# Attention over edge pairs: TensorE's two products change places, and VectorE instead of GpSimd copies the row numbers

## The chip, the cores and the metric

The kernel runs on one core of a Trainium2 chip. The metric is the device time of one launch in microseconds, the median of several runs; lower is better.

## The reference

A network of four graph layers on 6250 nodes and 206250 edges, in float32. The change is in the second layer, an attention over edges. For each edge, with features `m1` made from the rows of its two end nodes:

```
a   = sum(leaky(m1_s @ W_alpha).reshape(e, 4, 16) * alpha_dot, -1)     # logits, 4 heads
ex  = exp(a - segment_max(a, dst)[dst]); alpha = ex / segment_sum(ex, dst)[dst]
val = sigmoid(m1_s @ Ws_val), (m1_v @ Wv_val) * sigmoid(... @ Wg)
m2  = tensor_product(val, rsh)
h   = concat(m2_s @ Ws_vlin, m2_v @ Wv_vlin)                            # 4 heads x 40
agg = segment_sum(alpha * h, dst)
```

## The kernel before, in words

`edge_layer1` (phase name `e1`) does this with a running softmax. The edges stand in 1620 tiles of 128, taken as 810 pairs. For each of 12 tiles in turn there is a table in DRAM (`comb`) with a row per node: the node's mapped features, its maximum so far, and its sums so far. For each pair GpSimd gathers four blocks of 128 rows by indirect transfer (`srow` twice by source node, `crow` twice by destination node), and later writes two `crow` blocks back. The row numbers are columns of one int32 list in SBUF (`lists`); a small copy (L1095) puts the six columns of a pair into its slot of the ring `at` first.

Every engine runs the same loop, `run_steps`: a turn has six steps (`SLOTS`), written out, with 135 turns; the first `peel` turns are written out ahead of the loop. At the top of each turn an engine computes register values for its waits. In one step an engine works on several pairs at different stages: `s.back(k)` is the pair k steps older. The order inside a step is written by hand, and engines agree through counting semaphores. The stages of a pair that matter here:

- GpSimd: copy of row numbers in step s (L1095), four gathers one step later (L1076, L1079), two writes back five steps later (L1087), which wait for `kept` and `row_set`.
- VectorE (a = 2, b = 3, c = 4, r = 5 steps back): adds the gathered rows of a (L1320, `mv_set`); logits of b (L1323, L1326, `lg_set`); value products of b (L1331, `vv_set`); features of a (L1338 to L1352); maximum over the scores of b's first tile (L1357, waits for `x_lo`); accumulation of r (L1376, `row_set`); maximum for the second tile (L1394); new maximum (L1400), masks of a (L1406), differences (L1413).
- TensorE (a, b, c = 2, 3, 4 back): weights of a (`weights`, L1114); scores of b's first tile (`scores`, L1124 and L1127); the head maps of c (`second`, L1143 and L1145, 16 matmuls, `h_ps`); transposes of a (`turn`, L1120); scores of the second tile; and so on.

`second` writes PSUM bank `ps_h`, in which part of b's value matmuls (`VALS[1]`) also lie until VectorE has read them; so it waits for b's `vv_set`.

Of the kernel before, what the change touches and what calls it, by code (L numbers as in the profile page):

```python
# [6 lines left out]
I32 = mybir.dt.int32  # L7
# [975 lines left out]
def edge_layer1(nc, g, A, src_table, combs):  # L983
# [10 lines left out]
    def each(n):  # L994
        return [(16 * n, 16 * n * c) for c in (-1, 0, 1)]
    with Phase(nc, "e1") as ph:
        two = range(2)

        def ring(name, n, shape, dtype=F32):
# [3 lines left out]
        WvT, w2, adot = ph.sb("WvT", [64, P]), ph.sb("w2", [P, 2]), ph.sb("adot", [P, 4, 17])  # L1003
        straight, spare = ph.sb("straight", [P, CS]), ph.sb("spare", [P, 4, 16])
        ident16 = ph.sb("ident16", [P, P], BF16)
        keys, yt, at = ring("keys", SLOTS, [P, 2, P]), ring("yt", SLOTS, [P, 2, 10]), ring("at", SLOTS, [P, 6], I32)
        basis, comps = ring("basis", SLOTS, [P, P]), ring("comps", SLOTS, [P, P])
        srow, crow = ring("srow", 3, [P, 2, D]), ring("crow", SLOTS, [P, 2, COMB + 4])

# [13 lines left out]
        wl, made, wready, blank, straightened = (ph.sem(n) for n in ("weights", "made", "wready", "blank", "straightened"))  # L1023
        keys_in, mixed_in, yt_in = ph.sems_of("keys_in", SLOTS), ph.sems_of("mixed_in", SLOTS), ph.sems_of("yt_in", SLOTS)
        srow_in, crow_in, written = g.pool_dmas["e1"]
        (at_set, mixed_set, w_ps, w_read, mv_set, dup_set, cross_set, dots_set, feats1, m1_lo, m1_hi, m1T_lo, m1T_hi, a_ps,
         ra_set, th_set, lw_set, lg_set, vv_set, by_set, feats2, sv2_hi, sv2_lo, m2_lo, m2_hi, m2T_lo, m2T_hi, h_ps, masks, same_set,
         x_lo, x_hi, mx_lo, mx_hi, mn_set, dif_set, ex_set, kept, scaled, hw_set, g_ps, row_set) = (ph.sem(n) for n in (
             "at_set", "mixed_set", "w_ps", "w_read", "mv_set", "dup_set", "cross_set", "dots_set", "feats1", "m1_lo", "m1_hi", "m1T_lo",
             "m1T_hi", "a_ps", "ra_set", "th_set", "lw_set", "lg_set", "vv_set", "by_set", "feats2", "sv2_hi", "sv2_lo", "m2_lo", "m2_hi",  # L1030
             "m2T_lo", "m2T_hi", "h_ps", "masks", "same_set", "x_lo", "x_hi", "mx_lo", "mx_hi", "mn_set", "dif_set", "ex_set", "kept",
             "scaled", "hw_set", "g_ps", "row_set"))
# [1 line left out]
        def landed(n, times, more=0):  # L1034
            return n.value(16 * times, 16 * times * (n.off + 1 + more))

        def steps(eng, step, lag, held=()):
            run_steps(eng, step, lag, SLOTS, GROUPS, COUNTS + list(held))

        with nc.Block() as block:  # L1040
            @block.sync
            def _(sp):
# [23 lines left out]
            @block.gpsimd  # L1066
            def _(pool):
                def step(s):
                    n = s.back(1)
                    if n.exists():  # L1070
                        pool.wait_ge(wl, 16 * 9)
                        pool.wait_ge(at_set, n.count(1))
                        if n.reuses(3):
                            pool.wait_ge(mv_set, n.count(-2))
                        for q in two:
                            pool.indirect_dma_start(out=srow[n.j % 3][:, q, :], out_offset=None, in_=src_table,  # L1076
                                                    in_offset=bass.IndirectOffsetOnAxis(ap=at[n.j][:, q:q + 1], axis=0)).then_inc(srow_in[n.j], 16)
                        for q in two:
                            pool.indirect_dma_start(out=crow[n.j][:, q, 0:COMB], out_offset=None, in_=combs[2 * n.j + q][0:NP, :],  # L1079
                                                    in_offset=bass.IndirectOffsetOnAxis(ap=at[n.j][:, 2 + q:3 + q], axis=0)).then_inc(crow_in[n.j], 16)  # L1080
                    w = s.back(5)
                    if w.exists():
                        pool.wait_ge(wl, 16 * 9)
                        pool.wait_ge(kept, w.count(1))
                        pool.wait_ge(row_set, w.count(1))
                        for q in two:
                            pool.indirect_dma_start(out=combs[2 * w.j + q], out_offset=bass.IndirectOffsetOnAxis(ap=at[w.j][:, 4 + q:5 + q], axis=0),  # L1087
                                                    in_=crow[w.j][:, q, 0:COMB], in_offset=None).then_inc(written[w.j], 16)
                    if s.exists():
                        pool.wait_ge(wl, 16 * 9)  # L1090
                        if s.reuses(SLOTS):
                            pool.wait_ge(srow_in[s.j], landed(s, 2, -1))
                            pool.wait_ge(crow_in[s.j], landed(s, 2, -1))
                            pool.wait_ge(written[s.j], landed(s, 2, -1))
                        pool.tensor_copy(at[s.j][:, :].rearrange("p (k t) -> p k t", k=3),  # L1095
                                         g.lists[:, :].rearrange("p (k t) -> p k t", k=3)[:, :, bass.ds(s.t() * 2, 2)]).then_inc(at_set, 1)
                steps(pool, step, 5, each(2))
                for k in range(SLOTS):
                    pool.wait_ge(written[k], 32 * (GROUPS // SLOTS))

            @block.tensor
            def _(pe):
# [45 lines left out]
                def step(s):  # L1148
                    a, b, c = s.back(2), s.back(3), s.back(4)
                    if a.exists():  # L1150
                        weights(a)
                    if b.exists():
                        pe.wait_ge(masks, b.count(1))
                        pe.wait_ge(lg_set, b.count(1))
                        if b.reuses(1):
                            pe.wait_ge(mx_hi, b.count(0))
                        scores(b, 0, x_lo)
                    if c.exists():
                        pe.wait_ge(m2T_lo, c.count(1))
                        pe.wait_ge(m2T_hi, c.count(1))  # L1160
                        if c.reuses(1):
                            pe.wait_ge(hw_set, c.count(0))
                        if b.exists():
                            pe.wait_ge(vv_set, b.count(1))
                        second(c, 0)
                        second(c, 1).then_inc(h_ps, 1)
                    if a.exists():
                        pe.wait_ge(feats1, a.count(1))
                        if c.exists():
                            pe.wait_ge(m2T_lo, c.count(1))  # L1170
                            pe.wait_ge(m2T_hi, c.count(1))
                        turn(m1, a, 0, m1_lo)
                        turn(m1, a, 1, m1_hi)
                    if b.exists():
                        pe.wait_ge(mx_lo, b.count(1))
                        scores(b, 1, x_hi)
                    if a.exists():
                        pe.wait_ge(m1T_lo, a.count(1))
                        if b.exists():
                            pe.wait_ge(vv_set, b.count(1))  # L1180
                        first(a, 0)
                    if b.exists():
                        pe.wait_ge(feats2, b.count(1))
                        pe.wait_ge(sv2_hi, b.count(1))
                        if a.exists():
                            pe.wait_ge(m1T_hi, a.count(1))
                        turn(m2, b, 1, m2_hi)
                        pe.wait_ge(sv2_lo, b.count(1))
                        turn(m2, b, 0, m2_lo)
                    if a.exists():  # L1190
                        pe.wait_ge(m1T_hi, a.count(1))
                        if c.exists():
                            pe.wait_ge(hw_set, c.count(1))
                        first(a, 1).then_inc(a_ps, 1)
                    if c.exists():
                        pe.wait_ge(hw_set, c.count(1))
                        pe.wait_ge(kept, c.count(1))
                        pe.wait_ge(same_set, c.count(1))
                        if c.reuses(1):
                            pe.wait_ge(row_set, c.count(0))  # L1200
                        for q in two:
                            ins = pe.matmul(ps_g[:, q * 4 * HD:(q + 1) * 4 * HD], same[c.j % 2][:, q, :], hw[c.j % 2][:, q, :], start=True, stop=True)
                        ins.then_inc(g_ps, 1)
# [76 lines left out]
            def _(dve):  # L1280
# [32 lines left out]
                def step(s):  # L1313

                    q, a, b, c, r = (s.back(k) for k in (1, 2, 3, 4, 5))
                    ka, kb, kc = a.j % 2, b.j % 2, c.j % 2
                    if a.exists():
                        dve.wait_ge(srow_in[a.j], landed(a, 2))
                        dve.wait_ge(crow_in[a.j], landed(a, 2))
                        dve.tensor_tensor(mv[ka][:, :, 0:D], srow[a.j % 3][:, :, :], crow[a.j][:, :, 0:D], ALU.add).then_inc(mv_set, 1)  # L1320
# [51 lines left out]
                    if r.exists():  # L1372
                        dve.wait_ge(g_ps, r.count(1))
                        dve.wait_ge(scaled, r.count(1))
                        row = crow[r.j][:, :, D + 4:COMB]
                        dve.tensor_tensor(row, row, ps_g[:, 0:8 * HD].rearrange("p (t m) -> p t m", t=2), ALU.add).then_inc(row_set, 1)  # L1376
                    if q.exists():
# [803 lines left out]
```

## Time and profile before

| | us |
|---|---|
| median of 3 runs | 20541.54 (20539.68 to 20549.04) |
| profiled execution | 20573.62 |
| its span | 20572.0 |

| engine | busy us | share |
|---|---|---|
| TensorE matmul | 17578.1 | 85% |
| VectorE | 16081.1 | 78% |
| ScalarE | 12429.6 | 60% |
| GpSimd | 12351.1 | 60% |

The shares are over the whole span; the attention stage lies at about 5580 to 12980 us of it. Times of single instructions are from one profiled execution. A label "issue" behind a gap says that the profile shows nothing that the engine waited for.

### The profile page before, as it was taken

What the parts mean: (1) busy time and instruction counts of PE and PEld (TensorE: products, weight loads), DVE (VectorE), ACT (ScalarE), POOL (GpSimd) and SP (SyncE); (2) the same over time, 40 slices, a digit from 0 to 9 for tenths busy, and PEclk for the clock granted to TensorE, in tenths of its full rate; (3) what the DMA queues carried; (4) which work ended last, traced back from release to release, by engine and by line L of the source; (5) the groups of instructions that cost most, each with busy time, mean ns of one, the idle gap of its engine ahead of it and who ended that gap; (6) DMA issues with size and microseconds to landing.
All of it is one profiled execution on the core that took longest, in us unless ns stands there. A gap on an engine that the chain in (4) does not pass through costs nothing. (4 is left out here: it accounts for less than half of the span.)

```text
span 20572.0 us, 465117 instructions
## 1 busy us (share of the span) xinstructions
PE 17578.1 (85%) x121874; PEld 14135.8 (69%) x121874; DVE 16081.1 (78%) x44638; ACT 12429.6 (60%) x39738; POOL 12351.1 (60%) x13048
## 2 busy tenths in 40 slices
PE   2777666676699999999999999699998889999888
PEld 1333322222588888888888888699997669999766
DVE  3777799998588888888988888655556885555688
ACT  1222288887277777777777777267774226777422
POOL 2777777776367666666767676177772007777200
PEclk8888789888899999999999999999999999999999
DMA  2666577777744444444444444522222002222200
GB/s 83 170 171 171 164 136 142 140 141 127 240 121 123 122 121 122 122 121 122 124 123 123 122 121 122 140 64 67 67 67 30 6 6 63 67 67 67 30 6 6
DMA packets 1922898, 2132.27 MB, mean 104 GB/s; under 512 B 745584, under 2 KB 1597712, under 8 KB 1922544
## 3 DMA queue, kind: packets, MB, share of 16 engines
q0 software_dynamic: 567456, 1314.26, 24.1%
q1 hardware_dynamic: 1355344, 816.91, 16.1%
q8 instruction: 36, 0.59, 0.0%
q14 instruction: 62, 0.51, 0.0%
HBM read 1518.49 MB, written 611.44 MB: 104 GB/s over the span
## 5 line engine op out<-in xcount | busy, mean ns | idle before, releaser
L1639 POOL DMA_INDIRECT e_rows<-x,e_take x3456 | 3335.2, 965 | 1143.1 <-issue 1056.8
L1673 ACT ACTIVATE e_hot<-e_hot,e_here 128x128 f32<-128x128 f32 x10368 | 3123.5, 387 | 1389.2 <-DVE e_hot L1696 1381.3
L1659 PE MATMUL e_sums<-e_rows,e_hot 128*128 128x128 f32 x20736 | 2878.9, 275 | 0.0
L1659 PEld LDWEIGHTS e_sums<-e_rows,e_hot 128*128 128x128 f32 x20736 | 2678.9, 192 | 0.0
L632 PE MATMUL e_sums<-e_feat,e_same 128*128 128x480 f32 x3456 | 1761.3, 661 | 858.0 <-DVE e_feat L712 385.3
L615 POOL DMA_INDIRECT e_rows<-table,e_take x1728 | 1925.8, 1114 | 649.1 <-issue 620.9
L1214 ACT ACTIVATE e_m<-e_th,e_yt 128x64 f32<-128x64 f32 x6480 | 2301.3, 426 | 0.0
L1076 POOL DMA_INDIRECT e_srow<-src_table,e_at x1620 | 1615.2, 997 | 926.0 <-issue 917.8
L1087 POOL DMA_INDIRECT comb<-e_crow,e_at x1620 | 1664.6, 1028 | 823.7 <-issue 524.9
L771 POOL TENSOR_TENSOR n_stats<-n_stats,n_power 128x1 f32<-128x1 f32 x250 | 145.4, 582 | 3153.5 <-DVE n_stats L756 3066.4
L632 PEld LDWEIGHTS e_sums<-e_feat,e_same 128*128 128x128 f32 x3456 | 721.1, 219 | 1898.2 <-issue 1416.3
L1079 POOL DMA_INDIRECT e_crow<-comb,e_at x1620 | 1673.0, 1033 | 493.7 <-issue 449.2
L327 POOL DMA_INDIRECT pay_rows<-order_stage,order_put x1620 | 1582.3, 977 | 498.2 <-issue 370.2
L1120 PE MATMUL e_ps_m<-ident,e_m 128*128 128x128 f32 x12960 | 1808.6, 284 | 25.5 <-DVE e_m L1352 8.0
L1655 PE MATMUL e_sums<-e_rows,e_hot 128*128 128x160 f32 x6912 | 1580.1, 310 | 196.1 <-DMA e_rows<-x,e_take 111.7
L1696 DVE TENSOR_TENSOR e_hot<-e_iota,e_here 128x512 f32<-128x512 f32 x864 | 599.3, 694 | 1282.1 <-PE e_sums L1659 1282.1
L1120 PEld LDWEIGHTS e_ps_m<-ident,e_m 128*128 128x128 f32 x12960 | 1504.9, 150 | 84.4 <-DVE e_m L1352 10.0
L1656 PE MATMUL e_sums<-e_rows,e_hot 128*128 128x160 f32 x6912 | 1506.6, 300 | 0.0
L421 ACT ACTIVATE order_stage<-order_ps_w 128x448 f32<-128x448 f32 x810 | 441.8, 545 | 1505.8 <-PE order_ps_w L389 1502.6
L1145 PE MATMUL e_ps_h<-e_WV,e_m2T 128*128 128x32 f32 x9720 | 1317.9, 273 | 0.0
L658 ACT ACTIVATE e_feat<-e_feat,e_pay 128x64 f32<-128x64 f32 x5184 | 1280.7, 333 | 54.0 <-DVE e_feat L687 45.5
L1707 DVE TENSOR_TENSOR acc<-acc,e_sums 128x320 f32 x1728 | 843.3, 488 | 540.4 <-issue 289.1
(331 smaller groups left out, 46900.9 us busy)
## 6 DMA issues: line engine op xcount, KB each, us to landing
e_pay<-pay_rows SPq DMA_DIRECT2D x432, 470.0 KB
order_keys<-key_row SPq DMA_DIRECT2D x810, 128.0 KB
e_keys<-key_row SPq DMA_DIRECT2D x810, 128.0 KB, 3.4
comb<-n_comb SPq DMA_DIRECT2D x600, 164.0 KB, 2.0
e_rows<-x,e_take POOLq DMA_INDIRECT x3456
order_feat<-in_attr_T SPq DMA_DIRECT2D x810, 64.0 KB
e_basis<-in_attr_T SPq DMA_DIRECT2D x1620, 32.0 KB
e_comps<-in_attr_T SPq DMA_DIRECT2D x1620, 32.0 KB
```

The lines of the kernel that those rows point to most:

```text
L327: pool.indirect_dma_start(out=pay_rows, out_offset=bass.IndirectOffsetOnAxis(ap=put[t.j // 2][:, 2 * (t.j % 2) + q:2 * (t.j % 2) + q + 1], ...
L615: pool.indirect_dma_start(out=rows[t.j][:, q, 0:D], out_offset=None, in_=table, in_offset=bass.IndirectOffsetOnAxis(ap=take[t.j][:, q:q + ...
L632: ins = pe.matmul(sums[b][q // G][:, 0:AGG0], same[b][:, q, :], feat[b][:, q, 0:AGG0], start=q % G == 0, stop=q % G == G - 1)
L1076: pool.indirect_dma_start(out=srow[n.j % 3][:, q, :], out_offset=None, in_=src_table, in_offset=bass.IndirectOffsetOnAxis(ap=at[n.j][:, q: ...
L1079: pool.indirect_dma_start(out=crow[n.j][:, q, 0:COMB], out_offset=None, in_=combs[2 * n.j + q][0:NP, :], in_offset=bass.IndirectOffsetOnAx ...
L1087: pool.indirect_dma_start(out=combs[2 * w.j + q], out_offset=bass.IndirectOffsetOnAxis(ap=at[w.j][:, 4 + q:5 + q], axis=0), in_=crow[w.j][ ...
L1120: ins = pe.transpose(ps_m[q][:, c * P:(c + 1) * P], m[n.j % 2][:, q, c * P:(c + 1) * P], g.ident[:, :])
L1214: ins = act.activation(m2[k][:, q, c * P:c * P + CS], th[k][:, q, 0:CS], ACT.Identity, scale=y, bias=y)
L1639: pool.indirect_dma_start(out=rows[t.j][:, q, 0:D], out_offset=None, in_=x, in_offset=bass.IndirectOffsetOnAxis(ap=take[t.j][:, q:q + 1], ...
L1655: pe.matmul(to[:, 0:D], one[:, q, 0, :], row[:, q, 0:D], start=first, stop=last)
L1659: ins = pe.matmul(bass.AP(o.tensor, o.offset, [o.ap[0], [DOT - CS * c, 2], [1, CS]]), one[:, q, 2 + c, :], bass.AP(r.tensor, r.offset, [r. ...
L1673: ins = act.activation(one[:, q, 2 + c, :], one[:, q, 0, :], ACT.Copy, scale=here[t.j][:, q, TOWARDS + c:TOWARDS + c + 1])
```

## The change

On TensorE the block for c (`second`, with its waits, that for b's `vv_set` among them) is moved ahead of the block for b's first scores. GpSimd's copy goes. VectorE makes two copies instead, into two rings: `take` (the four columns for gathers) at the top of step s, and `place` (the two columns for the write back) behind its waits for the accumulation. GpSimd waits for `take_set`, and for the slot's earlier write back between the gathers of `srow` and of `crow`. Two of GpSimd's turns are written out ahead of its loop instead of one.

```diff
-        keys, yt, at = ..., ring("at", SLOTS, [P, 6], I32)
+        take, place = ring("take", SLOTS, [P, 4], I32), ring("place", SLOTS, [P, 2], I32)
+        lists = g.lists[:, :].rearrange("p (k t) -> p k t", k=3)
 # GpSimd
-                        pool.wait_ge(at_set, n.count(1))
+                        pool.wait_ge(take_set, n.count(1))
...                     (gathers of srow, by take)
+                        pool.wait_ge(wl, 16 * 9)
+                        if n.reuses(SLOTS):
+                            pool.wait_ge(written[n.j], landed(n, 2, -1))
...                     (gathers of crow, by take; writes back, by place)
-                    if s.exists():
-                        pool.wait_ge(wl, 16 * 9)
-                        if s.reuses(SLOTS):
-                            pool.wait_ge(srow_in[s.j], landed(s, 2, -1))
-                            pool.wait_ge(crow_in[s.j], landed(s, 2, -1))
-                            pool.wait_ge(written[s.j], landed(s, 2, -1))
-                        pool.tensor_copy(at[s.j]..., ...[:, :, bass.ds(s.t() * 2, 2)]).then_inc(at_set, 1)
-                steps(pool, step, 5, each(2))
+                steps(pool, step, 5, each(2), peel=2)
 # TensorE
-                    if b.exists():
-                        pe.wait_ge(masks, b.count(1))
-                        pe.wait_ge(lg_set, b.count(1))
-                        if b.reuses(1):
-                            pe.wait_ge(mx_hi, b.count(0))
-                        scores(b, 0, x_lo)
                     if c.exists():
...
                             pe.wait_ge(vv_set, b.count(1))
                         second(c, 0)
                         second(c, 1).then_inc(h_ps, 1)
+                    if b.exists():
+                        pe.wait_ge(masks, b.count(1))
+                        pe.wait_ge(lg_set, b.count(1))
+                        if b.reuses(1):
+                            pe.wait_ge(mx_hi, b.count(0))
+                        scores(b, 0, x_lo)
 # VectorE
+                    if s.exists():
+                        dve.tensor_copy(take[s.j]..., lists[:, 0:2, bass.ds(s.t() * 2, 2)]).then_inc(take_set, 1)
                     if a.exists():
                         dve.wait_ge(srow_in[a.j], landed(a, 2))
...
                         dve.wait_ge(scaled, r.count(1))
+                        dve.tensor_copy(place[r.j]..., lists[:, 2:3, bass.ds(r.t() * 2, 2)])
```

## Rows read from the trace of the kernel before

**Rows 1.** The page, whole span: busy us (share of the span) x instructions.
```profile
PE 17578.1 (85%) x121874; PEld 14135.8 (69%) x121874; DVE 16081.1 (78%) x44638; ACT 12429.6 (60%) x39738; POOL 12351.1 (60%) x13048
```

**Rows 2.** Windows, attention stage: length, busy us of PE, PEld, DVE, ACT, POOL, clock, DMA.
```profile
6000.00:12900.00 6900.00, 6598.08 (x50100) 5674.65 (x50099) 6164.86 (x18218) 5233.69 (x16699) 4813.26 (x5313) 0.98 0.41 122
```

**Rows 3.** Waits, 6000 to 12900 us: waiter <- releaser, us in total, times, longest.
```profile
POOL e_srow L1076 <- issue: 862.3, 1511, 1.5
...
DVE e_mv L1320 <- DMA e_crow<-comb,e_at: 481.6, 525, 2.9
...
POOL comb L1087 <- DVE e_crow L1376: 217.7, 145, 4.8
```

**Rows 4.** Groups by line, GpSimd, same stretch: busy us, mean ns | idle before.
```profile
L1095 POOL COPY e_at<-lists 128x6 int32 x759 | 173.4, 228 | 2.1
```

**Rows 5.** Timeline, GpSimd: start us, us, what [idle before <- releaser].
```profile
8362.33 0.20 POOL L1095 COPY e_at<-lists 128x6 int32 x1
8363.36 1.01 POOL L1076 DMA_INDIRECT e_srow<-src_table,e_at  x1 [0.82 <-issue]
8364.67 0.97 POOL L1076 DMA_INDIRECT e_srow<-src_table,e_at  x1 [0.31 <-issue]
...
8367.19 1.16 POOL L1079 DMA_INDIRECT e_crow<-comb,e_at  x1 [0.30 <-issue]
8369.54 1.00 POOL L1087 DMA_INDIRECT comb<-e_crow,e_at  x1 [1.19 <-DVE e_crow L1376]
...
8377.09 0.97 POOL L1079 DMA_INDIRECT e_crow<-comb,e_at  x1 [0.30 <-DVE e_crow L1376]
```

**Rows 6.** Timeline, VectorE, one step and the starts of the next two.
```profile
8362.57 0.49 DVE L1320 TENSOR_TENSOR e_mv<-e_srow,e_crow 128x320 f32<-128x320 f32 x1 [1.36 <-DMA e_crow<-comb,e_at]
...
8363.31 0.29 DVE L1326 TENSOR_REDUCE e_crow<-e_lw 128x8 f32<-128x136 f32 x1
...
8363.75 0.31 DVE L1331 SCALAR_TENSOR_TENSOR e_vv<-e_th,e_ps_h 128x160 f32<-128x160 f32 x1
...
8366.12 0.68 DVE L1357 TENSOR_REDUCE e_mx<-e_ps_x 128x4 f32<-128x512 f32 x1
...
8368.13 0.49 DVE L1376 TENSOR_TENSOR e_crow<-e_crow,e_ps_g 128x328 f32<-128x328 f32 x1
...
8370.14 0.16 DVE L1400 TENSOR_TENSOR e_mx<-e_crow,e_mx 128x8 f32<-128x8 f32 x1
8370.22 0.42 DVE L1406 TENSOR_TENSOR e_apart<-e_keys,key_f 128x256 bf16<-128x256 f32 x1
...
8370.64 0.48 DVE L1320 TENSOR_TENSOR e_mv<-e_srow,e_crow 128x320 f32<-128x320 f32 x1
...
8380.25 0.49 DVE L1320 TENSOR_TENSOR e_mv<-e_srow,e_crow 128x320 f32<-128x320 f32 x1 [1.10 <-DMA e_crow<-comb,e_at]
```

**Rows 7.** Timeline, TensorE (PE) and its weight loads (PEld), the same step.
```profile
8363.67 0.10 PEld L1124 LDWEIGHTS e_ps_x<-e_apart,e_ident 128*128 128x128 bf16 x1 [1.67 <-issue]
...
8363.92 0.60 PE L1127 MATMUL e_ps_x<-ident,e_crow 128*128 128x128 f32 x4
8364.25 0.30 PEld L1143 LDWEIGHTS e_ps_h<-e_WS,e_m2T 128*128 128x128 f32 x2
...
8371.22 1.13 PE L1114 MATMUL e_ps_w<-e_WY,e_mixed 64*128 64x512 f32 x4
```

**Rows 8.** Timeline, weight loads in another step: `second` and the transposes behind it.
```profile
8157.68 0.30 PEld L1143 LDWEIGHTS e_ps_h<-e_WS,e_m2T 128*128 128x128 f32 x2
...
8159.53 0.53 PEld L1120 LDWEIGHTS e_ps_m<-ident,e_m 128*128 128x128 f32 x5
```

**Rows 9.** Windows, two loop turns of VectorE; columns as in rows 2.
```profile
8308.25:8362.57 54.32, 52.80 (x398) 45.52 (x396) 48.89 (x144) 41.36 (x132) 37.14 (x42) 0.97 0.41 122
8362.57:8416.08 53.51, 51.27 (x398) 44.02 (x396) 48.59 (x144) 41.36 (x132) 37.60 (x42) 1.00 0.43 124
```

More of the change, by code:

```diff
@@ L1005, in edge_layer1 @@
         ident16 = ph.sb("ident16", [P, P], BF16)
-        keys, yt, at = ring("keys", SLOTS, [P, 2, P]), ring("yt", SLOTS, [P, 2, 10]), ring("at", SLOTS, [P, 6], I32)
+        keys, yt = ring("keys", SLOTS, [P, 2, P]), ring("yt", SLOTS, [P, 2, 10])
+        take, place = ring("take", SLOTS, [P, 4], I32), ring("place", SLOTS, [P, 2], I32)
         basis, comps = ring("basis", SLOTS, [P, P]), ring("comps", SLOTS, [P, P])
@@ L1025, in edge_layer1 @@
         srow_in, crow_in, written = g.pool_dmas["e1"]
-        (at_set, mixed_set, w_ps, w_read, mv_set, dup_set, cross_set, dots_set, feats1, m1_lo, m1_hi, m1T_lo, m1T_hi, a_ps,
+        (take_set, mixed_set, w_ps, w_read, mv_set, dup_set, cross_set, dots_set, feats1, m1_lo, m1_hi, m1T_lo, m1T_hi, a_ps,
          ra_set, th_set, lw_set, lg_set, vv_set, by_set, feats2, sv2_hi, sv2_lo, m2_lo, m2_hi, m2T_lo, m2T_hi, h_ps, masks, same_set,
          x_lo, x_hi, mx_lo, mx_hi, mn_set, dif_set, ex_set, kept, scaled, hw_set, g_ps, row_set) = (ph.sem(n) for n in (
-             "at_set", "mixed_set", "w_ps", "w_read", "mv_set", "dup_set", "cross_set", "dots_set", "feats1", "m1_lo", "m1_hi", "m1T_lo",
+             "take_set", "mixed_set", "w_ps", "w_read", "mv_set", "dup_set", "cross_set", "dots_set", "feats1", "m1_lo", "m1_hi", "m1T_lo",
              "m1T_hi", "a_ps", "ra_set", "th_set", "lw_set", "lg_set", "vv_set", "by_set", "feats2", "sv2_hi", "sv2_lo", "m2_lo", "m2_hi",
@@ L1035, in landed, with steps @@
             return n.value(16 * times, 16 * times * (n.off + 1 + more))
-        def steps(eng, step, lag, held=()):
-            run_steps(eng, step, lag, SLOTS, GROUPS, COUNTS + list(held))
+        def steps(eng, step, lag, held=(), peel=1):
+            run_steps(eng, step, lag, SLOTS, GROUPS, COUNTS + list(held), peel)
+        lists = g.lists[:, :].rearrange("p (k t) -> p k t", k=3)
         with nc.Block() as block:
@@ L1076, in step @@
                             pool.indirect_dma_start(out=srow[n.j % 3][:, q, :], out_offset=None, in_=src_table,
-                                                    in_offset=bass.IndirectOffsetOnAxis(ap=at[n.j][:, q:q + 1], axis=0)).then_inc(srow_in[n.j], 16)
+                                                    in_offset=bass.IndirectOffsetOnAxis(ap=take[n.j][:, q:q + 1], axis=0)).then_inc(srow_in[n.j], 16)
+                        pool.wait_ge(wl, 16 * 9)
+                        if n.reuses(SLOTS):
+                            pool.wait_ge(written[n.j], landed(n, 2, -1))
                         for q in two:
                             pool.indirect_dma_start(out=crow[n.j][:, q, 0:COMB], out_offset=None, in_=combs[2 * n.j + q][0:NP, :],
-                                                    in_offset=bass.IndirectOffsetOnAxis(ap=at[n.j][:, 2 + q:3 + q], axis=0)).then_inc(crow_in[n.j], 16)
+                                                    in_offset=bass.IndirectOffsetOnAxis(ap=take[n.j][:, 2 + q:3 + q], axis=0)).then_inc(crow_in[n.j], 16)
                     w = s.back(5)
@@ L1086, in step @@
                         for q in two:
-                            pool.indirect_dma_start(out=combs[2 * w.j + q], out_offset=bass.IndirectOffsetOnAxis(ap=at[w.j][:, 4 + q:5 + q], axis=0),
+                            pool.indirect_dma_start(out=combs[2 * w.j + q], out_offset=bass.IndirectOffsetOnAxis(ap=place[w.j][:, q:q + 1], axis=0),
                                                     in_=crow[w.j][:, q, 0:COMB], in_offset=None).then_inc(written[w.j], 16)
-                    if s.exists():
-                        pool.wait_ge(wl, 16 * 9)
-                        if s.reuses(SLOTS):
-                            pool.wait_ge(srow_in[s.j], landed(s, 2, -1))
-                            pool.wait_ge(crow_in[s.j], landed(s, 2, -1))
-                            pool.wait_ge(written[s.j], landed(s, 2, -1))
-                        pool.tensor_copy(at[s.j][:, :].rearrange("p (k t) -> p k t", k=3),
-                                         g.lists[:, :].rearrange("p (k t) -> p k t", k=3)[:, :, bass.ds(s.t() * 2, 2)]).then_inc(at_set, 1)
-                steps(pool, step, 5, each(2))
+                steps(pool, step, 5, each(2), peel=2)
                 for k in range(SLOTS):
@@ L1316, in step @@
                     ka, kb, kc = a.j % 2, b.j % 2, c.j % 2
+                    if s.exists():
+                        dve.tensor_copy(take[s.j][:, :].rearrange("p (k t) -> p k t", k=2), lists[:, 0:2, bass.ds(s.t() * 2, 2)]).then_inc(take_set, 1)
                     if a.exists():
@@ L1374, in step @@
                         dve.wait_ge(scaled, r.count(1))
+                        dve.tensor_copy(place[r.j][:, :].unsqueeze(1), lists[:, 2:3, bass.ds(r.t() * 2, 2)])
                         row = crow[r.j][:, :, D + 4:COMB]
```

## The prediction

> **What bounds the kernel now.** Read first the page's shares [rows 1]: TensorE is busy for 85% of the span and VectorE for 78%, but that is an average over several stages. The change lies in one of them, the attention stage, so the next view is the table of windows over that stage alone [rows 2]: in 6900 us TensorE is busy 6598, VectorE 6165, GpSimd 4813. GpSimd looks idle by 30%, but its gaps are not free time: the list of waits [rows 3] puts 862 us of them ahead of the first gather and calls them "issue". The copy of row numbers ran 759 times in that window [rows 4], so one step (one pair of tiles) takes 6900 / 759 = 9.09 us; six steps are one loop turn of 54.5 us, and 810 steps make 135 turns.
>
> Then GpSimd's queue in order of time [rows 5]. Each indirect transfer holds it about 1.0 us with a gap of 0.30 before the next; the copy takes 0.20 and the gap behind it is 0.82, because the gather waits for the copy that stands directly ahead of it. One step is six transfers (6 x 1.30 = 7.8) plus the copy's mean 0.23 [rows 4] and 0.52 of extra gap: 8.55 us of 9.09 with no other wait. So GpSimd is nearly a full queue, and VectorE's addition of the gathered rows pays for it: 482 us of waiting for the gather [rows 3], 0.63 us a step.
>
> VectorE's own pace is in [rows 6]: from the addition at 8362.57 to the next one at 8370.64, which found its data there, are 8.07 us. Once per turn 1.36 us stand ahead of the addition whatever the gather did (the loop's register work and branch; 8362.57 opens a turn). TensorE [rows 7] waits for the first scores' input (1.67 us at that turn start) and then runs without a break, from the weight load at 8363.67 to the end of the next pair's weight matmuls at 8371.22 + 1.13 = 8372.35: 8.68 us. So three engines lie within 8.1 to 8.7 us, and what one loses in order another must wait for.
>
> **The change part by part.**
>
> *Copy taken off GpSimd.* Its queue loses 0.23 + 0.52 = 0.75 us a step and needs about 7.8 us. What is late next is its write back, which waits for VectorE's accumulation (1.19 us at 8369.54, 0.92 us after that accumulation ended at 8368.62 [rows 5, 6]). The circle through it covers two steps: from an addition to the end of the accumulation 6.05 us, 0.92 to the first write, 2.3 for two writes, a gap of 0.30, the four gathers 4.99 (8363.36 to 8368.35 [rows 5]), and 2.19 until they land (end 8378.06, addition at 8380.25 [rows 5, 6]): 16.75 us, or 8.4 a step. The added wait for the earlier write back now stands ahead of the comb gathers, with them and the next writes queued behind it. That write was issued two GpSimd steps earlier instead of one, so it costs nothing; the second pair of waits on the weights is met once and for all. Peeling a second turn adds code, not steps.
>
> *Copies put on VectorE.* Two small ones a step. The trace has no such copy on VectorE. The nearest row is the 8-column maximum at L1400: the next instruction starts 0.08 us behind it [rows 6]. From below, 0 if the copy lies in a wait; from above, the 0.20 us of GpSimd's own copy each [rows 4]. I take 0.08 each, the row of the same engine: 0.16 a step, bounds 0 and 0.40. The first copy runs a whole step ahead of its reader, so no gather waits for it.
>
> *TensorE's order.* This is the expensive part. Before, the first scores of the middle pair wait for the logits: their weight load starts at 8363.67, 0.07 us behind the logits' end at 8363.60 [rows 6, 7]. The oldest pair's 16 matmuls then load from 8364.25. In the new order those come first, but they keep their wait for the middle pair's value products, which VectorE ends later, at 8363.75 + 0.31 = 8364.06 [rows 6]. They would start at 8364.13. They last 1.85 us (8157.68 to 8159.53 in a step where nothing held the transposes behind them [rows 8]), so the scores begin to load at 8365.98. Scores take 0.85 from first load to last end (8363.67 to 8364.52 [rows 7]): done at 8366.83, seen at 8366.90. VectorE wants them for its maximum at 8366.12 [rows 6]. Before they lay there 1.6 us early; now VectorE waits 0.78 us, in every step, and all that follows in its order moves back with it.
>
> What hides that? A TensorE that is late anyway, since then both orders start late. But in the new circle TensorE is early: 8.68 us of work against the sum below. Nor does the gather's wait absorb it, because that wait goes.
>
> *The sum.* VectorE's step: 8.07 + 0.78 + 0.16 = 9.01 us, more than GpSimd's 7.8. GpSimd's two-step circle gets the same delays ahead of its accumulation, 16.75 + 0.94 = 17.7 against 18.0, so it just does not bind. A turn: 6 x 9.01 + 1.36 = 55.4 us. To this comes the slow-clock cost of today's turns. The table by turns [rows 9] has one of 54.32 us at a granted clock of 0.97 and one of 53.51 at 1.00; the stage's mean clock is 0.98 [rows 2], which is 0.02 of time lost against 0.03 in such a turn, so some two turns in three; at 0.8 us each I put 0.6. The new turn is then 56.0 us against 54.5: 1.5 more, x 135 = 205 us. On the profiled execution's own 20573.62 us (span 20572.0 and 1.6 around it) that gives 20778; the median of the runs is 20541.54, 32 us below the profiled one, so the forecast is 20747 us.
>
> **The rivals.**
>
> *The low clock spreads to every turn* (slower still). After the turn-start gap TensorE's granted clock drops in some turns from the 2.4 to the 1.2 GHz level [rows 9]. The new order lengthens that gap: the first matmuls behind it move from 8363.67 to 8364.13, so 1.67 becomes 2.1 us [rows 7], and whatever runs slow next is now the 16 matmuls and the scores, exactly what VectorE waits for. At half clock their 2.7 us would be up to 5.4. If every turn pays 2.7 us instead of 0.6 on average: 2.1 x 135 = 284 us more, at the most; with half of that the time is about 20890. Against it: the turn with the 1.67 us gap at 8363.67 shows 1.00. In a sentence apart: the Trainium skill, "TensorE: Matmul & The Clock Gate", section "What's actually happening", says the throttled state is the default and activity releases it, so by it more idling means more slow turns; the trace agrees only so far that slow turns exist at 0.97 beside 1.00 [rows 9].
>
> *No change to speak of.* The 0.78 us replace the gather's 0.63, and VectorE's 1.36 us at the turn start vanish into the new wait because its sequencer gets ahead while VectorE stands still. Then a turn is 6 x 9.01 + 0.6 = 54.7, 0.2 more, 27 us: 20570. Against it: the maximum stands some ten instructions from the step's end, so the register work is reached long after the wait is over.
>
> *Faster.* TensorE decides instead: it is so late in every step that the value products are done before its weight matmuls end, and the order costs nothing, while GpSimd's 0.75 us come through. In the step of 8370.64 it is so: the weight matmuls end at 8372.35 [rows 7], and the value products, 1.49 behind the addition, at about 8372.13. Then TensorE's 8.68 us are the step: 52.1 + 1.36 + 0.6 = 54.0 if the turn start still adds fully, 52.7 if it lies beside; at the lower end 1.8 x 135 = 243 us off: 20300. It decides from the point where VectorE's step is under 8.68. Against it: the 0.78 us wait alone brings VectorE over that, and each wait of VectorE lets TensorE catch up.
>
> **How the numbers follow.** Forecast 0.56, low clock everywhere 0.20, no change 0.12, faster 0.12. A measurement of this kernel can tell about 0.2% (41 us) from no change, so faster 0.12, same 0.12, slower 0.76. The likeliest case's own range comes from the copies (0 to 0.40 a step, -130 to +194 us): 20617 to 20941. The range leaves out the faster case and the top of the slow-clock one: 20560 to 20980.
>
> **What would show it.** In the profile after: no copy on GpSimd and a gap of 0.30 instead of 0.82 ahead of the first gather; VectorE's wait for the gather under 0.2 us a step outside turn starts; in its place a wait of VectorE's first maximum for the scores, 0.7 to 0.9 us a step and some 600 us in all; TensorE's first load behind the weight matmuls 0.07 us after the value products. The forecast is wrong if the maximum does not wait, or if the wait for the gather stays.

## The result, and the profile after

The changed kernel takes 20952.43 us (median of 4 runs, 20938.33 to 20967.05) against 20543.28 us: ratio 1.0204, 95% interval 1.0191 to 1.0216. Slower, as forecast, but by 409 us and not by 205. Its profiled span is 20965.4 us.

All of it lies in the attention stage. These rows give first and last start of VectorE's additions, 810 in all, before and then after (duration min/median/max in ns ahead of them):

```profile
L1320 DVE TENSOR_TENSOR e_mv<-e_srow,e_crow x810: 477/492/583, 5596.2 to 12948.8; 128x320 f32<-128x320 f32 x162
```
```profile
L1319 DVE TENSOR_TENSOR e_mv<-e_srow,e_crow x810: 475/482/568, 5579.5 to 13342.7; 128x320 f32<-128x320 f32 x162
```

From first to last start, the 7352.6 us of the stage became 7763.2, 411 more: 9.09 us a step became 9.60, a turn of 54.5 us became 57.6. Beside the page's shares [rows 1] stands the page after; busy shares hardly move, so they don't explain anything:

```profile
PE 17943.8 (86%) x121874; PEld 14321.5 (68%) x121874; DVE 16240.5 (77%) x46258; ACT 12410.4 (59%) x39738; POOL 12184.6 (58%) x12238
```

The waits after, same stretch and columns as [rows 3]:

```profile
POOL comb L1092 <- DVE e_crow L1376: 894.2, 606, 3.4
...
DVE e_mx L1356 <- PE e_ps_x L1124: 541.8, 719, 2.7
...
POOL e_srow L1078 <- issue: 440.3, 1438, 0.6
...
DVE e_take L1315 <- issue: 167.7, 120, 1.4
...
DVE e_lw L1322 <- ACT e_ra L1227: 104.9, 103, 1.5
...
DVE e_mv L1319 <- DMA e_crow<-comb,e_take: 8.8, 15, 0.9
```

The wait for the gather has gone from 482 to 9 us, and GpSimd's queue now waits for VectorE. VectorE's maximum waits for the scores instead, in all 719 steps, 542 us. Each of 120 turns still has 1.40 us ahead of VectorE's first instruction. The table of windows, columns as in [rows 2], first the stretch of [rows 2], then two single turns as in [rows 9]:

```profile
6000.00:12900.00 6900.00, 6588.95 (x47467) 5543.69 (x47467) 5991.55 (x18703) 4941.05 (x15823) 4418.69 (x4316) 0.95 0.39 116
...
8212.73:8267.99 55.26, 52.54 (x396) 43.77 (x396) 49.93 (x158) 41.10 (x132) 36.75 (x37) 1.00 0.41 121
8427.07:8485.04 57.97, 55.52 (x398) 46.79 (x398) 50.00 (x158) 41.22 (x134) 36.97 (x36) 0.94 0.38 115
```

The clock column (third from the end: 1.00 is the 2.4 GHz level, 0.50 the 1.2 GHz level) is what the forecast did not have: 0.98 became 0.95. A turn at the 2.4 GHz level takes 55.26 us, one with a spell at the 1.2 GHz level 57.97. Counted by the trace's records of the granted clock over 115 turns in the middle of the stage, 100 have such a spell (mean 57.95 us) and 15 have none (55.22). In the kernel before, 48 of 115 have one (55.65 against 53.67). What happens in one, in order of time:

```profile
8437.40 0.17 DVE L1315 COPY e_take<-lists 128x4 int32 x1 [1.40 <-issue]
8437.51 0.49 DVE L1319 TENSOR_TENSOR e_mv<-e_srow,e_crow 128x320 f32<-128x320 f32 x1
...
8438.68 0.31 DVE L1330 SCALAR_TENSOR_TENSOR e_vv<-e_th,e_ps_h 128x160 f32<-128x160 f32 x1
...
8439.11 0.30 PEld L1140 LDWEIGHTS e_ps_h<-e_WS,e_m2T 128*128 128x128 f32 x2 [2.49 <-issue]
8439.14 0.41 PE L1140 MATMUL e_ps_h<-e_WS,e_m2T 128*128 128x64 f32 x2 [1.69 <-DVE e_vv L1330]
...
8441.81 0.29 PEld L1121 LDWEIGHTS e_ps_x<-e_apart,e_ident 128*128 128x128 bf16 x1
...
8443.52 0.69 DVE L1356 TENSOR_REDUCE e_mx<-e_ps_x 128x4 f32<-128x512 f32 x1 [2.38 <-PE e_ps_x L1124]
...
8448.19 0.48 DVE L1319 TENSOR_TENSOR e_mv<-e_srow,e_crow 128x320 f32<-128x320 f32 x1
8449.64 0.30 DVE L1322 TENSOR_TENSOR e_lw<-e_ra,e_adot 128x136 f32<-128x136 f32 x1 [0.97 <-ACT e_ra L1227]
```

VectorE's 1.40 us at the turn start make TensorE wait 1.69 us (2.49 us for the weight loads) until the value products are done at 8438.99. In the kernel before, where the scores came first, this gap in the matmuls was 0.87 us:

```profile
8363.70 0.38 PE L1124 MATMUL e_ps_x<-e_apart,e_ident 128*128 128x512 bf16 x1 [0.87 <-issue]
```

Behind the gap the changed kernel's TensorE runs slow: 16 matmuls take 2.70 us to the scores' first load (8439.11 to 8441.81), the maximum waits 2.38, and the next step's logits wait 0.97 more. The clock of that stretch, 0.52, shows that this was the 1.2 GHz level:

```profile
8439.50:8446.00 6.50, 6.50 (x32) 6.04 (x32) 4.08 (x12) 3.40 (x12) 1.98 (x3) 0.52 0.25 76
```

In a step at full clock 16 matmuls take 1.69 us (8410.82 to 8412.51) and the maximum waits 0.61:

```profile
8410.82 0.30 PEld L1140 LDWEIGHTS e_ps_h<-e_WS,e_m2T 128*128 128x128 f32 x2 [1.06 <-issue]
...
8412.50 0.36 DVE L1351 TENSOR_REDUCE e_m<-e_dots 128x64 f32<-128x192 f32 x1
8412.51 0.18 PEld L1121 LDWEIGHTS e_ps_x<-e_apart,e_ident 128*128 128x128 bf16 x1
...
8413.48 0.69 DVE L1356 TENSOR_REDUCE e_mx<-e_ps_x 128x4 f32<-128x512 f32 x1 [0.61 <-PE e_ps_x L1124]
```

### The profile page after: what moved, and what is told of

Same layout as the page of the kernel before. It is cut to its first block and busy times, and to the rows that moved or that the text cites. A ratio compares the mean times of both kernels' runs of the same rounds, so it can differ in the third digit from the quotient of the medians.

```text
span 20965.4 us, 465652 instructions
## 1 busy us (share of the span) xinstructions
PE 17943.8 (86%) x121874; PEld 14321.5 (68%) x121874; DVE 16240.5 (77%) x46258; ACT 12410.4 (59%) x39738; POOL 12184.6 (58%) x12238
## 5 line engine op out<-in xcount | busy, mean ns | idle before, releaser
L1092 POOL DMA_INDIRECT comb<-e_crow,e_place x1620 | 1821.5, 1124 | 1825.5 <-DVE e_crow L1376 1029.6
L1078 POOL DMA_INDIRECT e_srow<-src_table,e_take x1620 | 1592.1, 983 | 530.3 <-issue 501.2
L1084 POOL DMA_INDIRECT e_crow<-comb,e_take x1620 | 1562.3, 964 | 493.6 <-issue 493.3
L1117 PEld LDWEIGHTS e_ps_m<-ident,e_m 128*128 128x128 f32 x12960 | 1588.5, 153 | 14.4 <-DVE e_m L1351 11.7
L1142 PE MATMUL e_ps_h<-e_WV,e_m2T 128*128 128x32 f32 x9720 | 1400.1, 283 | 0.0
L1142 PEld LDWEIGHTS e_ps_h<-e_WV,e_m2T 128*128 128x128 f32 x9720 | 1308.6, 205 | 0.0
```

Source lines behind the costliest of these rows:

```text
L1117: ins = pe.transpose(ps_m[q][:, c * P:(c + 1) * P], m[n.j % 2][:, q, c * P:(c + 1) * P], g.ident[:, :])
L1142: ins = pe.matmul(heads[:, :, 16 + 8 * c:24 + 8 * c], mT[:, q, (c + 1) * P:(c + 2) * P], WV2[:, :], start=True, stop=True)
```

## The experiments

Theory: the wait for the value products, which now stands ahead of the scores, makes VectorE wait in each step, and lengthens TensorE's gap at the turn start so that the clock falls in nearly every turn; the copies by themselves gain. All ratios are to the kernel before on the same chip (its median differs by chip, 20543 to 20606 us). "Stage" is first to last start of VectorE's additions in the profile, as above.

| kernel | ratio, 95% interval | stage us |
|---|---|---|
| before | 1 | 7352.6 |
| changed | 1.0204 (1.0191 to 1.0216) | 7763.2 |
| copies alone | 0.9963 (0.9951 to 0.9976) | 7273.5 |
| order alone | 1.0248 (1.0231 to 1.0265) | 7840.5 |
| changed, gap filled (12) | 1.0060 (1.0044 to 1.0077) | 7467.4 |
| changed, gap half filled (5) | 1.0087 (1.0070 to 1.0104) | 7507.2 |
| changed, 12 in another step | 1.0193 (1.0176 to 1.0210) | 7732.6 |
| before, gap filled (7) | 0.9981 (0.9971 to 0.9990) | 7277.7 |
| own bank | 0.9968 (0.9955 to 0.9980) | 7274.4 |
| own bank, split | 0.9976 (0.9966 to 0.9986) | 7320.7 |
| copies alone, gap filled (9) | 0.9906 (0.9890 to 0.9923) | 7140.8 |
| own bank, split, filled (8) | 0.9904 (0.9887 to 0.9920) | 7131.7 |

**Each half alone.** The changed kernel with the scores' block back ahead of `second`; and the kernel before with the two blocks exchanged. The first as a diff to the changed kernel (the second is the same move, the other way round, in the kernel before):

```diff
+                    if b.exists():
...
+                        scores(b, 0, x_lo)
                     if c.exists():
...
                         second(c, 1).then_inc(h_ps, 1)
-                    if b.exists():
...
-                        scores(b, 0, x_lo)
```

> The changed kernel with TensorE's old order: the copies stay on VectorE. Theory (the order and the low clock that it brings are the whole loss, the copies alone are a gain): VectorE no longer waits for gathers, a step is 8.2 to 8.7 us, a loop turn 52.5 to 53.5 instead of 54.5, so 20280 to 20430 us; VectorE's first maximum doesn't wait for the scores, low clock in about half of the turns. Rival A (the copies on VectorE and the slower writes back of GpSimd are what costs): slower than before, over 20600 us.

> The kernel before with TensorE's new order alone; the copy stays on GpSimd. Theory: the whole loss comes from here and GpSimd's copy adds to it, since it lengthens the two-step circle through the write back to 16.75 + 0.78 + 0.75 = 18.3 us, 9.1 a step: 20940 to 21150 us, low clock in most turns. Rival A: the order costs little, so 20540 to 20700 us.

The order alone costs 2.5%; the copies gain 0.4%, in either order (1.0248 to 1.0204 is as much). Rival A falls. The gain of the copies is smaller than expected: a turn became 53.9 us (7273.5 / 809 x 6), not 52.5 to 53.5. The slow clock is enough to explain it: 70 of 115 turns have a spell, behind a gap of 1.08 us, and take 54.6 us against 53.0 for the others. Of VectorE's waits in this run the third, for ScalarE, goes when the gap is filled (below):

```profile
DVE e_mv L1319 <- DMA e_crow<-comb,e_take: 183.8, 265, 1.6
DVE e_take L1315 <- issue: 177.5, 127, 1.4
DVE e_lw L1322 <- ACT e_ra L1227: 84.1, 79, 1.2
```

**Filling the gap.** Transposes whose result nobody reads, in the first step of each turn of the changed kernel, ahead of `second`:

```diff
+                    if s.j == 0:
+                        for k in range(12):
+                            pe.transpose(ps_g[:, 384:512], g.ident[:, :], g.ident[:, :])
                     if c.exists():
```

> The changed kernel with 12 more transposes of the identity on TensorE (into columns of ps_g that nothing reads) in the first step of each loop turn, ahead of the oldest pair's values; about 1.4 us of work in a gap of some 1.7. Theory (the gap at the turn start lets the granted clock fall for the second step of nearly every turn, 2.7 us each): the low clock goes, a turn is 55.3 us instead of 57.6, so 20640 to 20720 us, with the wait of VectorE's first maximum still 0.5 to 0.6 us a step. Rival B (the clock falls because TensorE idles a little in every step, or has nothing to do with this gap): 20930 us or more.

More work on TensorE makes the kernel 1.4% faster. The clock stands at 1.00 and only 4 of 115 turns have a slow spell, none of them behind the filled gap; the wait for the scores is left:

```profile
6000.00:12900.00 6900.00, 6738.02 (x50867) 5623.88 (x50864) 6222.15 (x19448) 5127.09 (x16457) 4595.38 (x4490) 1.00 0.42 120
```
```profile
DVE e_mx L1359 <- PE e_ps_x L1124: 425.9, 746, 1.9
```

A turn is now 7467.4 / 809 x 6 = 55.4 us. Next the dose, and the place:

```diff
-                        for k in range(12):
+                        for k in range(5):
```
```diff
-                    if s.j == 0:
+                    if s.j == 3 and s.exists():
```

> The changed kernel with 5 transposes instead of 12 in the first step of each turn; about 0.6 us of the 1.66 us gap, so that some 1.1 us are left, as in the kernel with copies alone. Theory (it is the length of this gap that decides): low clock in some 60% of the turns and in single spells, 0.6 to 1.4 us a turn above the full fill: ratio 1.010 to 1.016. Rival (any transposes there do): 1.006; (none of them does, before the gap is filled): 1.020.

> The changed kernel with the 12 transposes in the fourth step of each turn instead of the first. Theory (only the long gap at the turn start matters): the low clock stays in nearly every turn and the transposes delay that step by 0.5 to 1.2 us: ratio 1.022 to 1.029. Rival B (more work anywhere keeps the clock up): 1.010 or less.

Five give most of it, a little more than expected: the clock is 0.99, and 38 of 115 turns have a slow spell. In another step the time stays about where it was, a shade below the expected range; but the clock did not stay at 0.95, which the theory had said:

```profile
6000.00:12900.00 6900.00, 6611.68 (x49082) 5570.56 (x49083) 6016.65 (x18767) 4955.98 (x15881) 4436.30 (x4332) 0.97 0.40 116
```

So work elsewhere spares some of the slow spells and pays it back in the step that it delays: turns with a spell are 73 of 115 instead of 100, but a turn without one takes 56.32 us instead of 55.22. In the gap the same 12 transposes cost such a turn 0.1 us (55.30).

The same in the old order, ahead of the scores (`range(7)` in the kernel before, `range(9)` in the copies alone):

```diff
+                    if s.j == 0:
+                        for k in range(9):
+                            pe.transpose(ps_g[:, 384:512], g.ident[:, :], g.ident[:, :])
                     if b.exists():
```

> The kernel before with 7 transposes of the identity in the first step of each turn, ahead of the scores; TensorE's gap there was 0.87 us. Theory (the forecast's 0.6 us of slow clock a turn was about right for the kernel before): low clock gone, 0.5 to 0.7 us a turn less, ratio 0.9954 to 0.9967. Rival (the price was too low already there): 0.993 or less.

> The changed kernel with TensorE's old order, and 9 transposes of the identity in the first step of each turn ahead of the scores; TensorE's gap there was 1.08 us. Theory (the turn-start gap lets the clock fall also in the old order, in some 60% of the turns, about 1.2 us each): ratio to before 0.991 to 0.994, low clock nearly gone. Rival B (the clock has nothing to do with this gap): 0.996 as without the transposes.

Filling gave the kernel before 0.19%, less than expected, or 0.3 us a turn (39 us / 135); by the stage in the profile it is 0.55 (75 us). 10 of 115 turns keep a slow spell, so this is a little less than the whole price. It gave the copies alone 0.6%, and none of their 115 turns has a spell; at 53.0 us (7140.8 / 809 x 6) a turn is then where the copies alone were expected. The order costs 2.4 us a turn at full clock ((7467.4 - 7140.8) / 135).

**The order or its wait.** `VALS[1]` moved to free columns of `ps_g`, so that `second` needs no `vv_set`; then halved around the scores; then 8 transposes ahead of the wait for `feats1` in the first step.

```diff
-        VALS = (..., ps_h[:, 8 * (HD - 1):8 * (HD - 1) + 5 * CV])
+        VALS = (..., ps_g[:, 8 * HD:8 * HD + 5 * CV])
...
-                        if b.exists():
-                            pe.wait_ge(vv_set, b.count(1))
                         second(c, 0)
...
+                            if k and r.exists():      # VectorE, ahead of the second value product
+                                dve.wait_ge(g_ps, r.count(1))
```

> The changed kernel, with the second tile's value matmuls in a free part of bank ps_g instead of ps_h; the oldest pair's values then need no wait for the middle pair's value products (VectorE's second value product waits for g_ps instead, which is done by then). The order of the change stays. Theory (not the order but its wait for the value products costs): the 16 matmuls start as soon as the weight matmuls end, lie in TensorE's gap, the scores come at 3 to 4 us after the addition and VectorE waits little; a turn of 52 to 53.5 us, 20200 to 20430 us. Rival C (it is the order itself): about 20950 us.

```diff
                         second(c, 0)
-                        second(c, 1).then_inc(h_ps, 1)
...
                         scores(b, 0, x_lo)
+                    if c.exists():
+                        second(c, 1).then_inc(h_ps, 1)
```

> The own-bank kernel with the 16 matmuls halved: the first tile's 8 ahead of the middle pair's scores, the second tile's 8 behind. Theory (what is left of VectorE's wait for the scores, 0.3 us in three steps of four, comes from the 1.85 us of matmuls ahead of them): the wait goes, ratio 0.990 to 0.996. Rival (TensorE's own work is the bound by now): 0.997 as without the split, and VectorE waits elsewhere.

```diff
-                        pe.wait_ge(feats1, a.count(1))
...
+                        if s.j == 0:
+                            for k in range(8):
+                                pe.transpose(ps_m[0][:, 0:P], g.ident[:, :], g.ident[:, :])
+                        pe.wait_ge(feats1, a.count(1))
```

> The split kernel with 8 transposes of the identity in the first step of each turn, ahead of the wait for the oldest features, where TensorE stood 1.2 us in the own-bank kernel. Theory (what low clock is left there goes): ratio 0.003 to 0.006 below the split kernel's. Rival: the same as the split kernel.

With the same order and no wait for the value products the loss is gone, 1.0204 to 0.9968: it was the wait, with the gap that it made. The gain over the kernel before is smaller than expected, 66 us (0.32% of 20543) where 113 was the least. The maximum still waits, up to 0.3 us, and TensorE, mostly at turn starts, waits for features:

```profile
DVE e_mx L1356 <- PE e_ps_x L1124: 167.1, 571, 0.3
PE e_ps_m L1117 <- DVE e_m L1351: 161.4, 140, 1.4
```

The split took away the maximum's wait and gained nothing, 0.9976, with the clock down to 0.97; filled, it is at 0.9904. That kernel and the copies alone with their gap filled beat the kernel before by 0.9 to 1.0%, and the changed kernel by 2.9%. The clock of the former up to the stage's end:

```profile
6000.00:12600.00 6600.00, 6508.85 (x50428) 5609.22 (x50428) 6173.33 (x19475) 5143.68 (x16478) 4582.55 (x4494) 1.00 0.44 126
```

The length of the gap alone does not say how often the clock falls. TensorE's longest gap in the first step of a turn is the same, within 0.05 us, in at least 106 of each kernel's 115 turns. The number of these turns in which a slow spell begins in that step is 35 at 0.87 us (before), 97 at 0.93 (own bank, split), 32 at 1.00 (half filled), 69 at 1.08 (copies alone), 34 at 1.18 (own bank) and 100 at 1.69 (changed). With the gap filled it is none, in each of the four kernels. What else decides stays open.

## Why the prediction was right in direction and half in size

- *GpSimd.* Right. No copy, a gap of 0.30 ahead of the first gather, gathers on time (9 us of waits) at the changed kernel's pace; at that of the copies alone VectorE waits 184 us for them again.

```profile
8369.01 0.99 POOL L1092 DMA_INDIRECT comb<-e_crow,e_place  x1 [0.30 <-issue]
8370.31 0.99 POOL L1078 DMA_INDIRECT e_srow<-src_table,e_take  x1 [0.30 <-issue]
```

- *The copies on VectorE.* Right at 0.16 a step: an instruction starts 0.07 behind the copy of places and 0.07 to 0.11 behind the other, though each shows 0.16 of duration.

```profile
8445.54 0.16 DVE L1374 COPY e_place<-lists 128x2 int32 x1
8445.61 0.48 DVE L1376 TENSOR_TENSOR e_crow<-e_crow,e_ps_g 128x328 f32<-128x328 f32 x1
```

- *TensorE's order.* Mechanism right, size a little high. The 16 matmuls start 0.12 us behind the value products, not 0.07, and take 1.69 us at full clock, not 1.85. In the step shown at full clock the maximum starts 0.98 us behind the instruction ahead of it (8412.50 to 8413.48). Before it was 0.28 (8365.84 to 8366.12):

```profile
8365.84 0.36 DVE L1352 TENSOR_REDUCE e_m<-e_dots 128x64 f32<-128x192 f32 x1
```

So the order costs that step 0.70 us where 0.78 was forecast. The profile's own wait, 0.61, counts only from the end of the instruction ahead. The mean wait of 0.75 (542 / 719) is that high because of the slow steps; in the filled kernel it is 0.57 (425.9 / 746).

- *The turn without low clock.* 55.4 us forecast; 55.26 in the turn shown, 55.4 in the filled kernel. So close a match is partly luck. By the starts of VectorE's instructions in the filled kernel the maximum's delay is 0.65 us a step on average, 0.8 us a turn less than forecast. About 0.5 of that comes back in what the sum left out: 0.4 where VectorE waits for the weight matmuls (L1111), and 0.1 more at the turn start.
- *The step that failed* is "I put 0.6" for the slow clock, taken from the turns of the kernel before and carried over unchanged into the new order. In the kernel before, filling gives back 0.3 to 0.55. In the changed kernel it gives back 2.2: the filled kernel's stage is 295.8 us shorter, / 135. With the forecast's own 55.4 that makes 57.6, the measured turn, and 57.58 - 54.53 = 3.05, x 135, is the 411 us found. The reading under the 0.6 was off too: "two turns in three" with 0.8 us each were 48 of 115 with 2.0 us on average. In the changed kernel they are 100 of 115 with 2.7. The rival *low clock in every turn* named this, its place and its price of 2.7 us a turn, and got 0.20. Its price was the 16 matmuls and the scores at half clock. In the slow turn shown it is 1.77 us more of the maximum's wait (2.38 against 0.61) and the 0.97 us of the next step's logits. It deserved more than 0.20, because the same edit makes the gap longer (0.87 to 1.69 us) and puts the matmuls that VectorE waits for right behind it.
- *No change* and *faster* fall. The turn start's 1.4 us did not vanish into the new wait, and TensorE was not late enough to hide the order: it waits for the value products (1.69 us at the turn start shown).

## What to carry to other kernels

A block that is moved ahead takes its waits with it, and what now stands behind it pays for them: before moving it, look at which of its waits ends last, here one that only a shared PSUM bank asked for. Where an edit lengthens an engine's regular gap, price the slow clock behind it anew and not at the old rate. On a TensorE with such a gap, a few idle transposes in it are worth a try: here 12 of them cost a turn at full clock 0.1 us and took 2.2 off the mean turn.

## What the runs showed of the hardware

In a stage where TensorE was busy 95% of the time, the granted clock fell to the 1.2 GHz level behind one gap of 0.9 to 1.7 us a turn, in 32 to 100 of 115 turns. Twelve transposes in the gap of 1.69 us left no spell behind it and took the stage's mean from 0.95 to 1.00. Ahead of VectorE's first instruction of a turn stand 1.36 to 1.40 us, in the kernel before, the changed one and the copies alone; the code has the turn's register work and branch there, and no run took them out. A small copy on VectorE shows 0.16 us of duration, but the next instruction starts 0.07 to 0.11 us behind its start.
